# Another order in the first DMA queues and on TensorE, and 8 picked rows in place of 14 for the second tile

## The chip, the cores and the metric

The kernel runs on one core of one Trainium2 chip. A core has TensorE (PE in the profile, its weight loads PEld), VectorE (DVE), ScalarE (ACT), GpSimd (POOL) and SyncE (SP), and 16 DMA engines. SP and ACT issue plain DMAs (SPq and ACTq in the rows), POOL issues the gathers. The metric is the device time of one launch in microseconds; smaller is better.

## The reference

A recommendation model for a batch of 1024. For each sample, 32 embedding rows of 16 floats are looked up in 32 tables, then three interaction layers follow, and a small tower on the sums:

```
e = stack([tbl_m[ids[:, m]] for m in range(32)], axis=1)            # (1024, 32, 16)
x0 = xk = e
for W in (W0, W1, W2):                                              # (32, 32 or 64, 64)
    xk = relu(einsum('bmd,bhd,mhk->bkd', x0, xk, W))
    outs.append(sum(xk, axis=2))
h = concatenate([concatenate(outs, 1), dense_ctx], 1)               # 3 * 64 + 16 = 208 wide
y = relu(relu(h @ W_top1 + b_top1) @ W_top2 + b_top2) @ W_top3
```

The tables have 1000, 1250, 12500 or 125000 rows. Everything is float32.

## The kernel before

**Tiles and phases.** The batch is cut into 8 tiles of 128 samples, each tile into two sides A and Bs of 64 samples. A phase is one layer of one side of one tile; `PHASES` lists all 48 in the order in which every engine goes through them. It begins (0, layer 0, A), (0, layer 1, A), (0, layer 0, Bs), (0, layer 2, A), (0, layer 1, Bs); the text calls these phases 0 to 4. A phase of layer 1 or 2 has 16 steps, a phase of layer 0 has 4.

**A step.** VectorE (L1110) multiplies a 128x1024 block of the current layer (`xk`, in PSUM) with a block of the replicated first layer (`x0rep`, in SBUF) into `z`, and TensorE (L753) contracts `z` with a block of the weights into `acc`. Some steps have their product made by GpSimd (L554, `z_pool`). `z` is a ring of 6 buffers, so VectorE can be 6 products ahead of TensorE. After a phase ScalarE takes `acc` through the relu into `xk_copy` (L861) and fills the two halves ("turns") of `xk` for a later phase: `fill_first` (L823) and `fill_second` (L842, L847). Phase 1 alone takes its first turn straight from `acc` (L831 on ScalarE, L1094 on VectorE).

**Where the embeddings come from.** GpSimd gathers rows with indirect DMAs (L504), one per table and tile, 32 per tile. At the start that would take long, so for tables of 1000 or 1250 rows the first two tiles are partly *picked*: SP and ACT load the whole table as 125 lines of 8 or 10 rows (L385, into the part of `x0rep` that is still free), and for each group of three or four tables TensorE spreads the line numbers over the partitions (`spread_lines`, L648), VectorE turns them into ones and zeros (`find_lines`, L1004), TensorE selects the lines by a product (`pick`, L662), and VectorE masks the other rows away and adds up (`find_rows` L1019, `clear_others` L1031, `take_rows` L1044). `PICKS` lists the groups: 6 for tile 0 (20 tables), then 4 for tile 1 (14 tables). The last three picks stand on VectorE between the four products of phase 0 (`between`).

**Saving and replicating.** The rows of a tile go from `emb` to DRAM (`x0_rows`; L457 for tile 0, L405 later) and are read back replicated as `x0rep` (L428, eight "slots" of 512 KB a side), as `lay` (L414) and as `squares` (L420). Tile 0 is saved in two parts: the even tables by `save_first(0)`, which waits for 3 pick groups, and the odd ones by `save_first(1)`, which waits for all 6. The even slots are loaded after the first part, the odd slots, on which the third product of phase 0 waits, after the second.

**Weights.** `w0` is symmetrised on VectorE (L1064), written to DRAM twice (L400, `w0_twice`) and read back rotated by 16 small loads (L379; `W0_LOADS` of them on ACT's queue, the rest on SP's). `w1` and `w2` are brought in by 8 direct loads (`STRAIGHT`) and 4 loads (`WRAPPED`) from a scratch copy in DRAM that two DMAs make first (`make_wrap`, L765); all of that is issued by ACT, the part for `w2` between two of its phases (L931 to L937). TensorE starts phase 1 only with all 12 loads of `w1` in, and phase 3 only with all of `w2`.

**What sets the order.** Each engine runs its own program in the order in which it is written, with semaphores between them. A DMA issued by SP or ACT stands in that engine's program like any other instruction: what is behind it waits until it is issued.

## Time and profile before

| | |
|---|---|
| median of 3 runs | 629.13 us (628.42 to 631.07) |
| profiled execution, its own time | 629.63 us |
| its span | 627.7 us |
| VectorE busy | 577.4 us, 92% |
| TensorE busy | 585.6 us, 93% |
| GpSimd busy | 497.3 us, 79% |
| ScalarE busy | 349.6 us, 56% |

The difference between the execution's own time and its span, 1.9 us, lies around the span. Busy time of TensorE is modelled. Read the table with the timeline beside it: an engine that is 92% busy over the whole span can still be mostly idle in its first tenth.

### The profile page before, as it was taken

The page shows a single profiled execution, that of the slowest core. Times are in us where ns is not written, and L with a number is a line of the kernel's source. Part 1 is how long each engine was busy: PE and PEld are TensorE (multiplying, and loading weights), DVE is VectorE, ACT ScalarE, POOL GpSimd, SP SyncE. Part 2 cuts the span into 40 slices and gives each one's busy share as a digit, 9 for nine tenths or more (in the row PEclk, how much of TensorE's full clock was granted, in tenths as well). Part 3 has the DMA queues.
Part 4 walks back from the last instruction along what each step waited for, and adds up shares of the span by engine and source line. Part 5 has one row for each costly group of instructions (what it writes and reads, how often), then busy time and mean ns, then how long its engine had stood idle before and what let it go on. Part 6 is the DMA issues. An engine that isn't in the chain of part 4 may idle for free. (4 is left out here: it accounts for less than half of the span.)

```text
span 627.7 us, 8728 instructions
## 1 busy us (share of the span) xinstructions
PE 585.6 (93%) x3126; PEld 214.1 (34%) x3126; DVE 577.4 (92%) x582; ACT 349.6 (56%) x535; POOL 497.3 (79%) x349
## 2 busy tenths in 40 slices
PE   3485689999999899999999999999999999999998
PEld 3361223222442224322342224322442234333444
DVE  5567599899999999999999999999999999999993
ACT  0105174745755667635755666635755666756741
POOL 6753579799888988899888988898888896668770
PEclk9879979999999999999999999999999999999999
DMA  4689979940499928993599727980699728990000
GB/s 110 129 165 236 251 119 272 294 118 4 77 237 224 191 19 185 231 240 58 81 243 247 159 28 198 296 210 3 114 236 242 138 28 202 237 247 3 1 2 1
DMA packets 89326, 95.36 MB, mean 152 GB/s; under 512 B 59597, under 2 KB 68338, under 8 KB 89282
## 3 DMA queue, kind: packets, MB, share of 16 engines
q1 hardware_dynamic: 78590, 90.55, 62.8%
q0 software_dynamic: 7104, 1.83, 3.9%
q10 hardware_dynamic: 3588, 2.41, 1.5%
q8 instruction: 25, 0.41, 0.3%
q14 instruction: 19, 0.16, 0.1%
HBM read 91.35 MB, written 3.94 MB: 152 GB/s over the span
## 5 line engine op out<-in xcount | busy, mean ns | idle before, releaser
L1110 DVE TENSOR_TENSOR z<-xk,x0rep 128x1024 f32<-128x1024 f32 x457 | 522.9, 1223 | 19.8 <-issue 9.6
L753 PE MATMUL acc<-z,w_sb 128*64 128x512 f32 x1828 | 433.6, 599 | 20.4 <-DVE z L1110 17.3
L554 POOL TENSOR_TENSOR z_pool<-x0rep,xk_copy 128x1024 f32<-128x1024 f32 x119 | 283.3, 2381 | 55.7 <-PE acc L753 27.9
L504 POOL DMA_INDIRECT emb<-tbl,idx x222 | 213.0, 959 | 58.4 <-issue 48.3
L753 PEld LDWEIGHTS acc<-z,w_sb 128*64 128x64 f32 x1828 | 123.7, 137 | 294.9 <-issue 161.2
L847 ACT ACTIVATE xk<-xk_copy 32x1024 f32<-32x1024 f32 x128 | 130.5, 1019 | 94.3 <-DVE z L1110 93.1
L753 PE MATMUL acc<-z_pool,w_sb 128*64 128x512 f32 x476 | 122.5, 593 | 0.0
L861 ACT ACTIVATE xk_copy<-acc 64x512 f32<-64x512 f32 x128 | 75.2, 588 | 3.7 <-PE acc L753 2.2
L842 ACT ACTIVATE xk<-lay 128x1024 f32<-128x1024 f32 x15 | 15.4, 1027 | 75.7 <-DVE z L1110 75.7
L753 PEld LDWEIGHTS acc<-z_pool,w_sb 128*64 128x64 f32 x476 | 33.7, 137 | 65.1 <-issue 62.8
L823 ACT ACTIVATE xk<-xk_copy 128x1024 f32<-128x1024 f32 x31 | 31.9, 1028 | 14.2 <-DVE z L1110 13.9
L1083 DVE TENSOR_REDUCE row_sums<-layer_out 128x32 f32<-128x512 f32 x47 | 32.2, 684 | 0.0
L805 ACT ACTIVATE squares<-squares 32x1024 f32<-32x1024 f32 x16 | 16.8, 1050 | 23.4 <-issue 14.5
L867 ACT ACTIVATE layer_out<-acc 128x512 f32<-128x512 f32 x47 | 27.8, 591 | 2.1 <-PE acc L753 1.4
L879 ACT ACTIVATE in<-row_sums 64x32 f32<-64x32 f32 x94 | 21.3, 227 | 4.7 <-DVE row_sums L1083 3.6
L1031 DVE TENSOR_TENSOR x0rep<-acc,mask 128x480 f32<-128x480 f32 (+1 forms) x10 | 6.7, 666 | 14.2 <-PE acc L662 14.2
L662 PE MATMUL acc<-x0rep 125*128 125x160 f32 (+1 forms) x68 | 14.8, 377 | 4.9 <-DMA x0rep<-tbl 4.9
L749 PE MATMUL acc<-squares,w0d_sb 128*64 128x512 f32 x64 | 16.9, 606 | 0.4
L823 ACT ACTIVATE xk<-lay 128x1024 f32<-128x1024 f32 x15 | 15.4, 1028 | 2.8 <-DMA lay<-x_rows 2.4
L784 ACT ACT_TABLE_LOAD x1 | 1.3, 1283 | 27.5 <-issue 27.5
L662 PEld LDWEIGHTS acc<-x0rep 125*128 125x128 f32 x68 | 12.6, 259 | 7.9 <-DMA x0rep<-tbl 5.3
L590 PEld LDWEIGHTS top<-h,wt_sb 128*64 128x64 f32 x224 | 12.7, 137 | 4.0 <-issue 4.0
(67 smaller groups left out, 140.6 us busy)
## 6 DMA issues: line engine op xcount, KB each, us to landing
x0rep<-x_rows SPq DMA_DIRECT2D x128, 512.0 KB, 20.7
lay<-x_rows SPq DMA_DIRECT2D x30, 512.0 KB, 6.9
emb<-tbl,idx POOLq DMA_INDIRECT x222, 3.5
squares<-x_rows SPq DMA_DIRECT2D x16, 128.0 KB, 8.6
x_rows<-emb SPq DMA_DIRECT2D x7, 256.0 KB, 4.6
x_rows<-emb SPq DMA_DIRECT2D x9, 128.0 KB, 5.9
w_wrap<-w ACTq DMA_DIRECT2D x4, 128.0 KB, 9.7
w_sb<-w ACTq DMA_DIRECT2D x8, 64.0 KB
```

What stands on the lines that cost most here:

```text
L504: pool.indirect_dma_start(out=emb[:, i % 2, m, :], out_offset=None, in_=tables[m], in_offset=bass.IndirectOffsetOnAxis(ap=idx[:, i, m:m + ...
L554: pool.tensor_mul(z_pool[:, (count - 1) % POOL_RING, :], x0rep[:, g % X0_GROUPS, slot, :], xk_copy[:, side, :]).then_inc(z_pool_ready, 1)
L662: op = pe.matmul(acc[:, ACC_AT[q], t * n * D:(t + 1) * n * D], hots[:, q % HOTS, t * P:(t + 1) * P], lines[:, ALL_PICKED.index(m), 0:n * D ...
L749: pe.matmul(bank[c * H:(c + 1) * H, :], w0d_sb[:], squares[:, side, c * COLS:(c + 1) * COLS], start=False, stop=False)
L753: mm = pe.matmul(bank[c * H:(c + 1) * H, :], w[:, tile, :], src[:, c * COLS:(c + 1) * COLS], start=(k == 0), stop=last)
L823: act.activation(xk[:, 0, :], src, ACT.Copy).then_inc(xk_ready[0], 1)
L847: op = act.activation(xk[q * Q:(q + 1) * Q, 1, :], xk_copy[other * Q:(other + 1) * Q, side, :], ACT.Copy)
L861: op = act.activation(xk_copy[half * H:(half + 1) * H, side, c * COLS:(c + 1) * COLS], bank[c * H:(c + 1) * H, :], ACT.Relu)
L867: act.activation(layer_out[:, n % OUTS, :], bank, ACT.Relu).then_inc(acc_taken, 1)
L879: op = act.activation(dst[:, at:at + ROWS], row_sums[c * H:(c + 1) * H, i % 2, row, :], ACT.Copy)
L1083: dve.tensor_reduce(row_sums[:, i % 2, SUM_ROWS.index((layer, side)), :], layer_out[:, n % OUTS, :].rearrange("p (b d) -> p b d", d=D), AX ...
L1110: dve.tensor_mul(z[:, (count - 1) % RING, :], xk[:, bank, :], src).then_inc(z_ready, 1)
```

## The change

It touches only what is issued in about the first 80 us of the program.

- *SP's queue*: the lines of pick groups 0 and 1 stand ahead of where they stood, and `w0_twice` ahead of the lines of groups 2 to 5. The indices of tile 1 come by a load of their own (`idx_second_in`), those of tiles 2 to 7 at the end of the first block. The two copies for `w1_wrap` come from ACT's queue to the end of that block, the two for `w2_wrap` from ACT's queue to the place ahead of the loads of side Bs. Two of the rotated `w0` loads move in between the first save and its wait, two more go to ACT (`W0_LOADS` 12).
- *ACT's queue*: of the eight direct `w1` loads four stand behind the second `copy_rows`, and the four wrapped ones behind the first `square`. The copies are gone from it.
- *TensorE*: `pick(3)`, `pick(4)` and `pick(5)` stand ahead of where they stood.
- *VectorE*: the ids of tile 1 are split after three picks instead of before the first.
- *Tile 1*: 8 tables picked (two groups) and 24 gathered, in place of 14 and 18.

```diff
-PICKS = [(0, g) for g in range(6)] + [(1, g) for g in range(4)]
+PICKS = [(0, g) for g in range(6)] + [(1, g) for g in range(2)]
...
-W0_LOADS = 10
+W0_LOADS = 12
...
             sp.dma_start(idx[:, 0, :], ids[0:P, :]).then_inc(idx_first_in, 16)
+            load_lines(sp, False, 0)
             for dst, src in ((w0a_sb, w0a), (w0b_sb, w0b)):
                 sp.dma_start(dst, src).then_inc(w0ab_in, 16)
-            load_lines(sp, False, 0)
-            sp.dma_start(idx[:, 1:NT, :], ids[P:B, :].rearrange("(t p) m -> p t m", p=P)).then_inc(idx_in, 16)
-            for g in range(1, len(PICKED)):
-                load_lines(sp, False, g)
+            sp.dma_start(idx[:, 1, :], ids[P:2 * P, :]).then_inc(idx_second_in, 16)
+            load_lines(sp, False, 1)
             sp.wait_ge(w0_summed, 2)
             for n in range(2):
                 sp.dma_start(w0_twice[:, n, :].rearrange("q (r t k) -> q r t k", r=M, t=TILES0), w0a_sb).then_inc(w0_twice_in, 16)
+            for g in range(2, len(PICKED)):
+                load_lines(sp, False, g)
+            make_wrap(sp, w1_wrap, w1, w1_wrap_in)
+            sp.dma_start(idx[:, 2:NT, :], ids[2 * P:B, :].rearrange("(t p) m -> p t m", p=P)).then_inc(idx_in, 16)
...
-                sp.wait_ge(saved_first, 32 * (odd + 1))
             save_first(0)
+            sp.wait_ge(w0_twice_in, 32)
+            load_w0(sp, W0_LOADS, W0_LOADS + 2)
+            sp.wait_ge(saved_first, 32)
             for slot in range(0, SLOTS, 2):
                 load_x0(0, A, slot)
-            load_w0(sp, W0_LOADS, TILES0 * P // M)
+            load_w0(sp, W0_LOADS + 2, TILES0 * P // M)
             save_first(1)
+            sp.wait_ge(saved_first, 64)
...
+            make_wrap(sp, w2_wrap, w2, w2_wrap_in)
             load_side(0, Bs)
...
@@ scalar
-            load_w0(act, 0, W0_LOADS - 2)
+            load_w0(act, 0, 8)
             copy_rows(0)
-            load_w0(act, W0_LOADS - 2, W0_LOADS)
-            make_wrap(w1_wrap, w1, w1_wrap_in)
-            load_w(w1_sb, w1.tensor, TILES, w1_in, STRAIGHT)
+            load_w0(act, 8, W0_LOADS)
+            load_w(w1_sb, w1.tensor, TILES, w1_in, STRAIGHT[:2])
             copy_rows(1)
-            act.wait_ge(w1_wrap_in, 32)
-            load_w(w1_sb, w1_wrap, WRAP, w1_in, WRAPPED)
+            load_w(w1_sb, w1.tensor, TILES, w1_in, STRAIGHT[2:])
...
             square(0, A)
+            act.wait_ge(w1_wrap_in, 32)
+            load_w(w1_sb, w1_wrap, WRAP, w1_in, WRAPPED)
...
                 if n == 1:
-                    make_wrap(w2_wrap, w2, w2_wrap_in)
@@ vector
-            dve.wait_ge(idx_in, 16)
-            split_ids(1)
             for q in range(7):
+                if q == 3:
+                    dve.wait_ge(idx_second_in, 16)
+                    split_ids(1)
                 pick_rows(q)
...
-            between = {1: 7, 2: 8, 4: 9}
+            between = {1: 7}
```

SP's queue from the first index load to the second save, before (`z<-w0a` is the load of `w0`, `w_twice` the doubled `w0`, `x0rep<-tbl` the lines of the picked tables, `x_rows<-emb` the two saves):

```order
L391 DMA idx<-ids 128x32
L393 DMA z<-w0a 128x256
L393 DMA z<-w0b 128x256
L385 DMA x0rep<-tbl 125x128 x2
L395 DMA idx<-ids 128x7x32
L385 DMA x0rep<-tbl 125x128 x2
L385 DMA x0rep<-tbl 125x160 x6
L400 DMA w_twice<-z 4x32x256 [waits w0_summed]
L400 DMA w_twice<-z 4x32x256
L457 DMA x_rows<-emb 128x16x16 [waits picked_out,gathered_first0]
L457 DMA x_rows<-emb 128x8x16
L428 DMA x0rep<-x_rows 128x1x1024 [waits saved_first]
```

The same stretch of SP's queue now:

```order
L398 DMA idx<-ids 128x32
L392 DMA x0rep<-tbl 125x128 x2
L401 DMA z<-w0a 128x256
L401 DMA z<-w0b 128x256
L402 DMA idx<-ids 128x32
L392 DMA x0rep<-tbl 125x128 x2
L406 DMA w_twice<-z 4x32x256 [waits w0_summed]
L406 DMA w_twice<-z 4x32x256
L392 DMA x0rep<-tbl 125x160 x6
L385 DMA w_wrap<-w 128x256 x2
L410 DMA idx<-ids 128x6x32
L467 DMA x_rows<-emb 128x16x16 [waits picked_out,gathered_first0]
```

The two scratch copies of `w1` and the indices of tiles 2 to 7 now stand directly ahead of the first save; the large index load no longer stands ahead of the lines of group 1.

ScalarE from the first `copy_rows` to the take-over of phase 0, before:

```order
L784 ACTIVATE lay<-xk 16x1024 [waits rows_turned]
L379 DMA w_sb<-w_twice 16x2x64 x2
L765 DMA w_wrap<-w 128x256 x2
L776 DMA w_sb<-w 64x1x256 x2
L776 DMA w_sb<-w 32x1x256 x4
L776 DMA w_sb<-w 64x1x256 x2
L784 ACTIVATE lay<-xk 16x1024 [waits rows_turned]
L776 DMA w_sb<-w_wrap 32x1x256 [waits w1_wrap_in]
L776 DMA w_sb<-w_wrap 32x1x256 x3
L805 ACTIVATE squares<-squares 32x1024 [waits rows_in0]
L831 ACTIVATE xk<-acc 64x512 [waits step_done]
```

And now:

```order
L789 ACTIVATE lay<-xk 16x1024 [waits rows_turned]
L380 DMA w_sb<-w_twice 16x2x64 x4
L781 DMA w_sb<-w 64x1x256 x2
L781 DMA w_sb<-w 32x1x256 x2
L789 ACTIVATE lay<-xk 16x1024 [waits rows_turned]
L781 DMA w_sb<-w 32x1x256 x2
L781 DMA w_sb<-w 64x1x256 x2
L808 ACTIVATE squares<-squares 32x1024 [waits rows_in0]
L781 DMA w_sb<-w_wrap 32x1x256 [waits w1_wrap_in]
L781 DMA w_sb<-w_wrap 32x1x256 x3
L836 ACTIVATE xk<-acc 64x512 [waits step_done]
```

The four wrapped `w1` loads have moved behind an ACTIVATE that waits for the squares of the second save.

ScalarE between the second turn of phase 1 (the `xk<-xk_copy` rows) and phase 2 (the `squares` and `lay` rows), before:

```order
L847 ACTIVATE xk<-xk_copy 32x1024 x3
L765 DMA w_wrap<-w 128x256 x2
L776 DMA w_sb<-w 64x1x256 [waits x0_in0_7]
L776 DMA w_sb<-w 64x1x256
L776 DMA w_sb<-w 32x1x256 x4
L776 DMA w_sb<-w 64x1x256 x2
L776 DMA w_sb<-w_wrap 32x1x256 [waits w2_wrap_in]
L776 DMA w_sb<-w_wrap 32x1x256 x3
L937 DMA in<-ctx_t 16x128
```

And now:

```order
L852 ACTIVATE xk<-xk_copy 32x1024 x3
L781 DMA w_sb<-w 64x1x256 [waits x0_in0_7]
L781 DMA w_sb<-w 64x1x256
L781 DMA w_sb<-w 32x1x256 x4
L781 DMA w_sb<-w 64x1x256 x2
L781 DMA w_sb<-w_wrap 32x1x256 [waits w2_wrap_in]
L781 DMA w_sb<-w_wrap 32x1x256 x3
L941 DMA in<-ctx_t 16x128
L808 ACTIVATE squares<-squares 32x1024 [waits rows_in1]
```

The two copies are gone from here, and the semaphore `w2_wrap_in` on which the wrapped loads wait is now raised by copies that SP issued earlier.

## Rows read from the trace of the kernel before

**Rows 1.** The page: busy time of each engine, its share and instructions.

```profile
PE 585.6 (93%) x3126; PEld 214.1 (34%) x3126; DVE 577.4 (92%) x582; ACT 349.6 (56%) x535; POOL 497.3 (79%) x349
```

**Rows 2.** Timeline, VectorE, 35 to 120: start, duration, operation, idle before.

```profile
35.42 0.66 DVE L1031 TENSOR_TENSOR x0rep<-acc,mask 128x480 f32<-128x480 f32 x1 [9.87 <-PE acc L662]
...
48.37 2.36 DVE L1110 TENSOR_TENSOR z<-xk,x0rep 128x1024 f32<-128x1024 f32 x2 [0.36 <-DMA x0rep<-x_rows]
...
54.22 4.62 DVE L1110 TENSOR_TENSOR z<-xk,x0rep 128x1024 f32<-128x1024 f32 x4
61.53 5.75 DVE L1110 TENSOR_TENSOR z<-xk,x0rep 128x1024 f32<-128x1024 f32 x5 [2.69 <-issue]
...
67.79 3.48 DVE L1110 TENSOR_TENSOR z<-xk,x0rep 128x1024 f32<-128x1024 f32 x3
78.15 4.62 DVE L1110 TENSOR_TENSOR z<-xk,x0rep 128x1024 f32<-128x1024 f32 x4 [6.88 <-issue]
82.97 9.14 DVE L1110 TENSOR_TENSOR z<-xk,x0rep 128x1024 f32<-128x1024 f32 x8 [0.20 <-ACT xk L823]
```

**Rows 3.** Timeline, ScalarE and its DMA issues (ACTq), 20 to 100.

```profile
41.88 2.60 ACTq L776 DMA_DIRECT2D w_sb<-w_wrap  x4
49.55 1.05 ACT L805 ACTIVATE squares<-squares 32x1024 f32<-32x1024 f32 x1 [6.66 <-DMA squares<-x_rows]
...
56.88 0.56 ACTq L765 DMA_DIRECT2D w_wrap<-w  x1
...
60.96 3.11 ACTq L776 DMA_DIRECT2D w_sb<-w  x4
68.05 2.60 ACTq L776 DMA_DIRECT2D w_sb<-w_wrap  x4
70.68 5.23 ACTq L937 DMA_DIRECT2D in<-ctx_t  x1
...
78.94 2.38 ACT L861 ACTIVATE xk_copy<-acc 64x512 f32<-64x512 f32 x4
```

**Rows 4.** Timeline, DMA issues of SP, 0 to 60.

```profile
20.20 1.39 SPq L457 DMA_DIRECT2D x_rows<-emb  x2
24.42 3.66 SPq L428 DMA_DIRECT2D x0rep<-x_rows  x4
...
37.91 2.63 SPq L457 DMA_DIRECT2D x_rows<-emb  x2
42.94 0.55 SPq L428 DMA_DIRECT2D x0rep<-x_rows  x1
43.52 0.67 SPq L420 DMA_DIRECT2D squares<-x_rows  x1
```

**Rows 5.** Windows: stretch, busy times, TensorE clock, DMA share, GB/s.

```profile
18.00:20.00 2.00, 0.29 (x3) 0.05 (x1) 2.00 (x5) 0.00 (x0) 1.39 (x2) 1.00 0.31 100
26.00:38.00 12.00, 6.51 (x20) 3.29 (x21) 2.41 (x6) 2.29 (x2) 9.02 (x10) 0.53 1.00 222
...
42.00:44.00 2.00, 2.00 (x17) 1.35 (x18) 1.93 (x5) 0.88 (x1) 0.82 (x1) 1.00 0.06 18
46.00:77.00 31.00, 20.46 (x90) 5.88 (x88) 21.65 (x24) 10.28 (x13) 14.36 (x9) 1.00 1.05 245
```

**Rows 6.** The page, DMA issues: count, size, median us to landing.

```profile
x0rep<-x_rows SPq DMA_DIRECT2D x128, 512.0 KB, 20.7
```

**Rows 7.** Timeline, TensorE, 72 to 90.

```profile
72.30 1.03 PE L753 MATMUL acc<-z,w_sb 128*64 128x512 f32 x4
79.52 5.39 PE L753 MATMUL acc<-z,w_sb 128*64 128x512 f32 x12 [6.19 <-DVE z L1110]
...
87.36 2.79 PE L753 MATMUL acc<-z,w_sb 128*64 128x512 f32 x12 [0.70 <-DMA w_sb<-w_wrap]
```

**Rows 8.** Timeline, GpSimd, 40 to 160.

```profile
39.97 0.94 POOL L504 DMA_INDIRECT emb<-tbl,idx  x1 [0.30 <-issue]
...
56.84 2.37 POOL L554 TENSOR_TENSOR z_pool<-x0rep,xk_copy 128x1024 f32<-128x1024 f32 x1 [12.71 <-ACT xk_copy L861]
```

23 lines of the change are left out of this document (10 added, 13 removed).

## The prediction

> **What bounds the kernel now.** I read the page first. VectorE is 92% and TensorE 93% busy [rows 1], so over the whole span the two products per step leave no room, and the change removes none of them. What can move is idle time near the start. The second view is VectorE's timeline up to 120 us: it shows where the most loaded engine still waits [rows 2]. Three waits matter. At 35.42 it has been idle 9.87 us for the last pick of tile 0. At 61.53 it waits 2.69 us for ScalarE to fill the second turn of phase 1; nothing in the change touches that. At 78.15 it starts phase 2 after 6.88 us of idle. From 82.97, where phase 3 starts, it hardly stops. So the result is read from two marks: S, the start of phase 1 (54.22), and T, the start of phase 3 (82.97). What T moves by, the end moves by, since everything behind it is released by the same engines in the same order.
>
> The third view, ScalarE's timeline, explains 78.15 [rows 3]: from 56.88 ScalarE issues w2's two copies, then eight loads until 64.07 (60.96 + 3.11), then waits until 68.05 for the copies to land, then issues four more and the context load until 75.91 (70.68 + 5.23). Only then come the squares and the fill of phase 2. The fourth, SP's issues, gives the chain before S [rows 4]: second save issued at 37.91, landed at 42.94, slot 1 issued there, third product at 48.37 after a wait of 0.36 us for that slot [rows 2]; then two products, the last step of phase 0 on TensorE, the turn-over, and S. From slot 1's issue to S it is 54.22 - 42.94 = 11.3 us. The fifth view, the windows, tells that DMA is full from 26 to 38 (share 1.00, 222 GB/s), nearly empty from 42 to 44 (0.06), and full again from 46 to 77 (1.05) [rows 5].
>
> **The change, part by part.** My working starts from the profiled execution, 629.63 us (span 627.7 and 1.9 around it), 0.5 above the median of 629.13.
>
> *Picks.* Two groups fewer, and the last pick of tile 0 is not behind `select_rows(0)` any more. That takes the 9.87 us wait away: following VectorE, with the durations that the operations have now, the sixth group would be done at about 26 us instead of 37.84. This is no gain by itself, because the save it releases stands in SP's queue behind other transfers. The two picks dropped (8 and 9) lie between products of phase 0 that wait for slot 1 anyway. I cost all of this at 0; with the DMA cover gone it is the first rival.
>
> *Six more gathers.* One takes 0.94 and a gap of 0.30 [rows 8], so 6 x 1.25 = 7.5 us of GpSimd, against the 12.71 us that it now stands idle before its first product. Cost 0; the cover left is 5 us.
>
> *First save.* SP can issue it somewhat earlier than now (20.20), but the rings are still busy then: from 18 to 20 table lines are still being moved at 100 GB/s [rows 5], and their amount is unchanged. The copies of w1, 2 x 128 KB, now stand ahead of the save: 0.26 MB at 222 GB/s are 1.2 us. So the even slots start at 24.42 + 1.2 = 25.6. Bounds: if the save did not queue at all it would land 4.2 us (24.42 - 20.20) after an issue at about 18, that is at 22, 2.4 us sooner than now; at the other end two copies at 100 GB/s cost 2.6 us. I take +1.2, since a transfer issued into a busy queue lands late here (median 20.7 us for a slot [rows 6]).
>
> From 18 to 20 the DMA share is 0.31 at a time when almost only table lines are moving [rows 5]. The Trainium skill ("DMA: Bandwidth & Descriptors", section on why a DMA increments its semaphore by 16 and not by 1) says that a transfer is spread over the largest number of engines up to 16 that divides both outer dimensions; a table of 125 lines gets 5, and 5 of 16 is 0.31, so the trace agrees. By that rule the save queues on those five engines only; by an even spread the queue would be empty and the first term would be the 22 us bound, 3.6 us better than what I take.
>
> *Second save.* SP issues it at about 30.5 now (25.6, four slots in 3.66 [rows 4], two small loads), far ahead of 37.91. But the even slots are ahead of it in the same queue. From 26 to 38 DMA moved 12 us x 222 GB/s = 2.7 MB: four even slots (2.1), two copies (0.26), eight w1 loads (0.38). Now the copies are gone and four of the w1 loads (0.19) are issued later: 0.45 MB less, 2.0 us. Drained at 38 + 1.2 - 2.0 = 37.2, the save landed 4.2 us later (as the first did), at 41.4: 1.5 us sooner than 42.94. Slot 1 then has no wrapped w1 loads beside it (41.88 now [rows 3]), 128 KB or 0.5 us. Sum for S: -2.0, S = 52.2. Bounds: -7 (the first rival) and +1.4 (2.6 for the copies, none of the 2.0 given back, minus the 1.2 counted, is 42.94 + 1.4).
>
> *Wrapped w1 loads.* They were issued at 41.88 into an empty stretch. Now they follow the squares of tile 0, which were taken up at 49.55, 6.0 us after their issue at 43.52; with slot 1 at 41.4 they are issued from 48.0, into the full stretch. TensorE wants them at S + 1.3 = 53.5. How long they take there no row tells directly. Nearest above: w2's wrapped loads, issued at 68.05, released TensorE at 87.36, 19.3 us later, but with eight loads still ahead of them. Nearest below: 6.0 us for the squares. I take 8, nearer to the lower end, because the queue ahead is short: TensorE starts phase 1 at 56.0, after some 5 us of idle. After such an idle it runs at half clock: three steps (12 records) took 5.39 us from 79.52 after 6.19 us of waiting, against 2.79 us for three from 87.36 [rows 7]. So 5.4 + 13 x 0.93 = 17.5 us, and phase 1 ends on TensorE at 73.5. VectorE is not held up, it can be 6 products ahead.
>
> *w2 off ScalarE's path.* Two issues (1.2 us) and the wait for the copies (64.07 to 68.05, 4.0) go. ScalarE has the rest issued at 75.91 - 5.2 - 2.0 = 68.7 or sooner, and VectorE ends phase 1 at S + 17.05 = 69.3 (71.27 now [rows 2]). So phase 2 follows at once, or within 1.5 us, and the 6.88 us wait goes almost whole. What is late next is the take-over of phase 1 for phase 3: now L861 starts at 78.94 and VectorE's phase 3 4.0 us later, at 82.97. It now has to wait for TensorE's end of phase 1 (73.33 in the old trace, no bound there [rows 7]). T = 73.5 + 4.0 = 77.5, that is -5.5. Bounds of T - S, 28.75 now: 23.1 with w1 in time (19.1 + 4.0), 28.75 with nothing won.
>
> *w2's landing.* TensorE starts phase 3 now at 87.36, after waiting for the last of w2 [rows 7], 30.5 us after 56.88, with 768 KB on ACT's queue. Now 512 KB from about 55: by bytes 20.3 us, 75 to 76; by transfers, 12 of 14, 26.1 us, 81. It is wanted at T + 1.2 = 78.7. I take 0.5 us of loss out of a range of 0 to 2.3.
>
> Sum: -5.5 + 0.5 = -5.0; 629.63 - 5.0 = 624.6 for the profiled execution, 624.1 against the median.
>
> **The rivals.**
>
> *First: the start is won whole.* If the second save overtakes the even slots in the queue, it lands about 5.5 us after 30.5, slot 1 is issued at 36 instead of 42.94 and S moves by -6.9 to 47.3. The wrapped w1 loads then come early too, T - S is 23.1, T = 70.4 (-12.6); w2, wanted at 72 and there at about 74, takes 2 back: -10.6, 618.5. GpSimd allows it: 24 gathers of 1.25 us after the first twelve end near 49, its first product is wanted at S + 2.6 = 49.9. For it speaks that the picks really are done at 26; against it the 20.7 us of [rows 6]. The Trainium skill (same page, "Queues, rings and completion order") has descriptors of one queue consumed in order on each engine, and the semaphore raised only after every earlier write of that engine: by that this rival falls, and no row here shows two transfers overtaking.
>
> *Second: the start gains nothing and w2 becomes the wait.* The copies of w1 cost 2.6 us, S stays at 54.2, and phase 3 on TensorE starts at 84.9 instead of 87.36 because the wrapped loads of w1 are ahead of w2 in ACT's queue. Result -2.5, 626.6: no change that can be told. For it: the full DMA stretch from 46 on, in which the same bytes have to move in any order.
>
> *Third, the slower side: the wrapped w1 loads are as late as w2's.* With 19.3 us instead of 8 they release TensorE at 67.3; phase 1 ends at 84.8, T = 88.8, +5.9, 635.0. The place is TensorE's first product of phase 1; it decides from a landing 13.4 us after issue (release at 61.4, phase 1's end at 78.9, T at 82.97 as now). Against it: in their place there is little ahead on ACT's queue. For it: SP's queue is as full as it was then. By the Trainium skill's rule on the number of engines, cited above, such a load with an outer dimension of 4 runs on 4 of the 16 engines, which makes long landings likelier; no row here shows single engines.
>
> **How the numbers follow.** Forecast (S -2, T -5 to -6): 0.52, own range 620.5 to 627. First rival 0.13. Second 0.24. Third, with milder forms of it, 0.11. Predicted 624.1. The range, 617.5 to 630, holds the first two rivals and leaves most of the third out. 0.5% is 3.1 us, about what a measurement of this kernel can tell from no change: faster means below 626.0. Of the forecast 0.45 lies there, all of the first rival, 0.04 of the second: 0.62. Slower (above 632.3) is most of the third: 0.09. The rest, 0.29, is the same.
>
> **What would show it.** Second save: SP's first odd slot at 41.4 (rival one: 36; rival two: 43 or later). S at 52.2. VectorE's wait before phase 2 under 2 us. TensorE's first product of phase 1 released by the w1 loads, not by VectorE, at about 56, and at half clock; rival three has it at 67. T at 77.5, TensorE's phase 3 at 79 to 81. GpSimd idle before its first product some 5 us. From phase 3 on the trace should be the old one, shifted. The forecast is wrong if S moves by more than 5 us, if VectorE still waits over 4 us before phase 2, or if a new wait for x0rep or for gathered rows appears in phases 3 to 8.

## The result, and the profile after

After 633.53 us (median of 7 runs, 632.22 to 634.11), before on the same chip 630.17 us (median of 7, 628.42 to 632.04): ratio 1.0047, 95% interval 1.003 to 1.0064. That is 0.5% slower, small but clear of the noise. The forecast was 624.1 us, five below the kernel before, with a range of 617.5 to 630; it came out three above the kernel before. The execution whose profile follows took 634.11 us, span 632.3.

VectorE's timeline after, in the columns of [rows 2]:

```profile
48.06 2.36 DVE L1114 TENSOR_TENSOR z<-xk,x0rep 128x1024 f32<-128x1024 f32 x2 [11.39 <-DMA x0rep<-x_rows]
54.77 1.42 DVE L1098 TENSOR_SCALAR xk<-acc 64x512 f32<-64x512 f32 x2 [4.36 <-PE acc L764]
56.23 4.62 DVE L1114 TENSOR_TENSOR z<-xk,x0rep 128x1024 f32<-128x1024 f32 x4
63.54 2.36 DVE L1114 TENSOR_TENSOR z<-xk,x0rep 128x1024 f32<-128x1024 f32 x2 [2.69 <-issue]
69.01 1.23 DVE L1114 TENSOR_TENSOR z<-xk,x0rep 128x1024 f32<-128x1024 f32 x1 [3.11 <-PE acc L764]
...
74.00 8.07 DVE L1114 TENSOR_TENSOR z<-xk,x0rep 128x1024 f32<-128x1024 f32 x7
87.47 9.14 DVE L1114 TENSOR_TENSOR z<-xk,x0rep 128x1024 f32<-128x1024 f32 x8 [5.40 <-ACT xk L828]
```

S, the start of phase 1, is 56.23 (54.22 before), T, the start of phase 3, 87.47 (82.97). The wait of 6.88 us before phase 2 is gone: the seven products from 74.00 run without a gap from the end of phase 1 through phase 2. But 3.11 us appear inside phase 1 and 5.40 before phase 3, both for TensorE in the end. Its own timeline, with [rows 7] to compare:

```profile
39.76 3.68 PE L764 MATMUL acc<-z,w_sb 128*64 128x512 f32 x8 [4.36 <-DMA w_sb<-w_twice]
49.34 1.98 PE L764 MATMUL acc<-z,w_sb 128*64 128x512 f32 x4 [5.90 <-DVE z L1114]
...
67.00 6.95 PE L764 MATMUL acc<-z,w_sb 128*64 128x512 f32 x20 [12.27 <-DMA w_sb<-w_wrap]
...
89.37 2.79 PE L764 MATMUL acc<-z,w_sb 128*64 128x512 f32 x12 [1.69 <-DMA w_sb<-w_wrap]
```

TensorE stood idle 12.27 us for a wrapped load of w1 and began phase 1 at 67.00. ScalarE and its queue (against [rows 3]) tell when that load was issued:

```profile
49.31 1.06 ACT L808 ACTIVATE squares<-squares 32x1024 f32<-32x1024 f32 x1 [15.90 <-DMA squares<-x_rows]
49.32 2.60 ACTq L781 DMA_DIRECT2D w_sb<-w_wrap  x4
...
64.39 7.08 ACTq L781 DMA_DIRECT2D w_sb<-w_wrap  x4
71.51 2.56 ACTq L941 DMA_DIRECT2D in<-ctx_t  x1
...
83.43 2.40 ACT L866 ACTIVATE xk_copy<-acc 64x512 f32<-64x512 f32 x4 [4.88 <-PE acc L764]
```

Issue at 49.32, release 17.7 us later; the take-over of phase 1 starts at 83.43 as soon as TensorE is through, and phase 3 follows 4.04 us behind. SP's issues (against [rows 4]) and the windows (against [rows 5]: stretch, busy times, TensorE's granted clock, DMA share, GB/s):

```profile
21.08 1.39 SPq L467 DMA_DIRECT2D x_rows<-emb  x2
...
25.33 3.54 SPq L438 DMA_DIRECT2D x0rep<-x_rows  x4
...
30.40 8.60 SPq L467 DMA_DIRECT2D x_rows<-emb  x2
42.57 0.55 SPq L438 DMA_DIRECT2D x0rep<-x_rows  x1
```

```profile
18.00:20.00 2.00, 2.00 (x9) 1.92 (x8) 1.22 (x4) 0.00 (x0) 1.39 (x3) 1.00 0.86 225
26.00:38.00 12.00, 9.38 (x64) 5.88 (x64) 8.44 (x15) 1.01 (x1) 9.00 (x10) 0.85 1.01 205
42.00:44.00 2.00, 1.44 (x4) 0.00 (x0) 0.00 (x0) 0.00 (x0) 1.39 (x3) 0.50 0.19 21
46.00:77.00 31.00, 15.39 (x48) 4.71 (x50) 17.92 (x17) 11.32 (x14) 17.12 (x12) 0.64 1.05 230
```

The second save is issued 7.5 us earlier than before and lands 0.4 us earlier. DMA is as full from 46 to 77 as before (1.05), and TensorE's mean clock in that stretch is 0.64 where it was 1.00. GpSimd, against [rows 8]:

```profile
48.73 0.94 POOL L518 DMA_INDIRECT emb<-tbl,idx  x1 [0.30 <-issue]
58.85 2.35 POOL L569 TENSOR_TENSOR z_pool<-x0rep,xk_copy 128x1024 f32<-128x1024 f32 x1 [9.18 <-ACT xk_copy L866]
```

From T to the end of the span it is 544.8 us, before 544.7. The two agree so closely partly by chance. The shift against before is 4.5 us at T, but ScalarE's take-overs show 3.8 at 195.61 (before: 191.84), 2.4 at 217.16 (214.74) and 4.5 again at 289.66 (285.15). In between each kernel waits for a landing of `x0rep` that the other does not wait for, first before, then after:

```profile
207.82 11.41 DVE L1110 TENSOR_TENSOR z<-xk,x0rep 128x1024 f32<-128x1024 f32 x10 [1.11 <-DMA x0rep<-x_rows]
```

```profile
280.50 1.23 DVE L1114 TENSOR_TENSOR z<-xk,x0rep 128x1024 f32<-128x1024 f32 x1 [1.01 <-DMA x0rep<-x_rows]
282.74 11.41 DVE L1114 TENSOR_TENSOR z<-xk,x0rep 128x1024 f32<-128x1024 f32 x10 [1.01 <-DMA x0rep<-x_rows]
```

Fourteen of the twenty profiles of this document have such waits behind 150 us, of 0.2 to 1.1 us each and at changing places. So a mark near the start tells the end of a single profile to 1 or 2 us, not better.

### The profile page after: what moved, and what is told of

Same layout as the page of the kernel before. It is cut to its first block and busy times, and to the rows that moved or that the text cites. A ratio compares the mean times of both kernels' runs of the same rounds, so it can differ in the third digit from the quotient of the medians.

```text
span 632.3 us, 8682 instructions
## 1 busy us (share of the span) xinstructions
PE 586.2 (93%) x3108; PEld 213.3 (34%) x3108; DVE 573.3 (91%) x572; ACT 349.9 (55%) x535; POOL 502.9 (80%) x355
## 5 line engine op out<-in xcount | busy, mean ns | idle before, releaser
L1114 DVE TENSOR_TENSOR z<-xk,x0rep 128x1024 f32<-128x1024 f32 x457 | 523.3, 1226 | 33.2 <-DMA x0rep<-x_rows 13.7
L518 POOL DMA_INDIRECT emb<-tbl,idx x228 | 218.7, 959 | 58.2 <-issue 50.9
L808 ACT ACTIVATE squares<-squares 32x1024 f32<-32x1024 f32 x16 | 16.8, 1051 | 29.3 <-DMA squares<-x_rows 18.4
L677 PE MATMUL acc<-x0rep 125*128 125x128 f32 (+1 forms) x56 | 13.2, 408 | 5.8 <-DMA x0rep<-tbl 5.8
L760 PE MATMUL acc<-squares,w0d_sb 128*64 128x512 f32 x64 | 17.7, 631 | 0.3
L605 PE MATMUL top<-h,wt_sb 128*64 128x128 f32 x224 | 13.4, 273 | 0.0
## 6 DMA issues: line engine op xcount, KB each, us to landing
squares<-x_rows SPq DMA_DIRECT2D x16, 128.0 KB, 19.3
```

Source lines behind the costliest of these rows:

```text
L518: pool.indirect_dma_start(out=emb[:, i % 2, m, :], out_offset=None, in_=tables[m], in_offset=bass.IndirectOffsetOnAxis(ap=idx[:, i, m:m + ...
L605: last = pe.matmul(top[halves[half], m * P:(m + 1) * P], wt2_sb[:, k, columns_of(m, half)], h1[:, k, :], start=(k == 0), stop=(k == F1 // ...
L677: op = pe.matmul(acc[:, ACC_AT[q], t * n * D:(t + 1) * n * D], hots[:, q % HOTS, t * P:(t + 1) * P], lines[:, ALL_PICKED.index(m), 0:n * D ...
L1114: dve.tensor_mul(z[:, (count - 1) % RING, :], xk[:, bank, :], src).then_inc(z_ready, 1)
```

## The experiments

Eighteen more runs followed in five groups; the kernels of a group share one chip and its runs of the kernel before. The chips were of two kinds. On the chips of two groups the kernel before takes 630 us, as on the first one; on three it takes 654 to 656, and there TensorE is held up some 20 us in the picks (last section). I call them the 630 and the 654 chips; ratios are each against before on the same chip. The marks of all profiles, to which the paragraphs below refer (us from the span's start; "w1" is the issue of its first wrapped load and TensorE's first product of phase 1, V where VectorE released it; "PE 3" TensorE's first product of phase 3, "~" where it is read inside a merged row):

```
                       slot 1    S      w1 issue, first product     T      PE 3    span    ratio
630 chips
before                 42.94   54.22   41.88   55.59  V           82.97   87.36   627.7
after                  42.57   56.23   49.32   67.00  17.7        87.47   89.37   632.3   1.0047
eight_picked_alone     43.47   57.48   40.88   58.84  V           86.01  ~88.8    629.9   1.0022
top_later_alone        43.38   54.69   42.15   56.06  V           81.16  ~84.6    625.4   0.9989
skewed_top_later       42.28   55.53   48.90   58.94  10.0        79.19   84.12   624.6   0.998
both_and_top_later     42.79   54.29   41.32   55.66  V           79.18   81.89   622.1   0.9972
after_ten_picks_2      43.76   56.81   49.85   66.32  16.5        87.01   89.80   630.5   1.0045
all_mended_2           41.76   54.61   47.77   56.83   9.1        77.82   82.93   623.9   0.997
654 chips
before_marks           67.10   79.92   64.26   81.30  V          107.89 ~110.6    653.6
after_marks            67.18   78.51   73.42   90.19  16.8       110.30  115.74   661.2   1.0064
w1_before_square       66.28   78.17   70.88   91.82  20.9       112.57  113.94   658.1   1.0062
w1_before_square_2     64.97   77.52   70.23   92.16  21.9       111.62  113.00   657.7   1.0085
w1_behind_square       68.73   81.22   74.98   94.27  19.3       114.59  115.96   661.0   1.006
w1_loads_plain_rows    65.51   78.24   71.70   85.03  13.3       104.44  112.62   659.7   1.0019
w2_copies_by_sp        68.99   82.47   65.00   83.84  V          105.67  114.55   657.9   1.0034
after_skewed           67.17   78.47   73.28   83.00   9.7       103.37  110.63   655.3   1.002
w2_by_sp_skewed        64.70   75.93   63.50   77.30  V           99.14  108.43   653.8   1.0004
after_filled           66.06   90.31   72.24   94.01  21.8       114.31  115.69   660.4   1.0087
after_ten_picks        58.36   71.36   64.67   80.63  16.0       101.17  105.08   648.8   0.9959
all_mended             57.45   70.23   63.47   73.28   9.8        93.43   98.55   641.9   0.9844
```

My theory for the first four runs below: the late wrapped loads of w1 end phase 1 (rival three), and the rest of the change gains what it should. Its rival: w2, or the DMA volume, binds anyway. Each profile is one execution, and slot 1 moves by over 4 us between profiles of kernels with the same first queues on the 654 chips, so single marks are read against the nearest row and the ratios against their intervals.

**w1_behind_square.** The kernel before with w1's wrapped loads alone moved, as the change has them:

```diff
             copy_rows(1)
-            act.wait_ge(w1_wrap_in, 32)
-            load_w(w1_sb, w1_wrap, WRAP, w1_in, WRAPPED)
...
             square(0, A)
+            act.wait_ge(w1_wrap_in, 32)
+            load_w(w1_sb, w1_wrap, WRAP, w1_in, WRAPPED)
```

> The kernel before with the other part alone: its four wrapped w1 loads stand behind the square of tile 0 (issue near 49.6 instead of 41.9). Theory: they release TensorE 15 to 19 us after issue, near 66 instead of 55.6, at half clock, phase 1 ends on TensorE near 83, T near 87, so 4 us slower than before, 634. Rival (in the changed kernel the loads were late because of the copies of w2 and w1 on SP's queue): release near 58, T as before, no change in time.

659.95 us, ratio 1.006 (1.0029 to 1.0091). This one edit is slower by about as much as the whole change (3.9 us in the medians, 3.4 and 4.3 for the whole). TensorE's release, 19.3 us after the issue:

```profile
94.27 6.79 PE L753 MATMUL acc<-z,w_sb 128*64 128x512 f32 x20 [14.56 <-DMA w_sb<-w_wrap]
```

**w1_before_square** and, on another chip, **w1_before_square_2**: the kernel after with the same two lines moved back ahead of `square(0, A)`.

> The changed kernel with one thing put back: the four wrapped w1 loads are issued ahead of the square of tile 0 (right behind the other four direct ones, near 35 us) instead of behind it (49.32). Theory (the loads, issued 14 us later into full DMA queues, cost the time): TensorE's first product of phase 1 waits for VectorE and not for w1, at S + 1.3; phase 1 ends on TensorE near S + 19, T = S + 23 to 24, that is 79 to 80 in place of 87.5, and the whole is about 7 us faster than the changed kernel, 626 to 627, and 0.4 to 0.7% faster than before. Rival (the loss is in the start itself: cold TensorE, late slot 1, and the w1 loads only take the blame): T stays over 84 and the time within 2 us of the changed kernel's 633.5.

> The kernel w1_before_square again, for a chip on which the second layout is ready before slot 1 is issued: there the four wrapped loads of w1 are issued at about 35 in place of 49, ahead of the odd x0 slots. Theory (the loads are late since they stand behind the odd slots and side B): they are down before phase 0 ends, TensorE starts phase 1 with VectorE's first product at about 57, T at about S + 25, and what is left is w2's hold before phase 3: ratio 0.998 to 1.003 against after's 1.005. Rival (these loads are late wherever they stand): release over 15 us after issue or TensorE's first product of phase 1 after 60, ratio 1.004 to 1.007.

659.92 us, 1.0062 (1.0036 to 1.0089), and 659.24 us, 1.0085 (1.0052 to 1.0118). Both fell on 654 chips, where the second layout is late, so that the loads came out only some 5 us behind slot 1's issue, and not 14 us earlier as meant. There they took 20.9 and 21.9 us and released TensorE no sooner than in after_marks (91.82 and 92.16 against 90.19, on three chips). A place 1 to 1.6 us nearer to the issue of slot 1, but still behind it, gains nothing; what an issue well ahead of the slots would do in the new order stays untested. In the old order the loads are issued 1.1 to 4.0 us ahead of slot 1 (all rows with V), and in all of them VectorE released TensorE, 14 to 19 us after the issue; when the loads had landed these rows do not show.

**w1_loads_plain_rows.** The kernel after, w1's wrapped loads reading 32 plain rows instead of 4 groups of 8. The rows then come from other tiles of the scratch copy, so this kernel leaves out part of `w1`; it serves for the time alone.

```diff
                         rows = bass.AP(src, ((odd * H + h) * tiles + t) * H,
+                                       [[tiles * H, (hi - lo) * PER_GROUP], [1, half * H]] if plain else
                                        [[(PER_GROUP * tiles + 1) * H, hi - lo], [tiles * H, PER_GROUP], [1, half * H]])
...
-            load_w(w1_sb, w1_wrap, WRAP, w1_in, WRAPPED)
+            load_w(w1_sb, w1_wrap, WRAP, w1_in, WRAPPED, plain=True)
```

> The changed kernel with the wrapped w1 loads reading the same number of bytes as plain rows (32 rows of 1 KB, one outer dimension of 32 on both sides, in place of 4 groups of 8 rows); they read other tiles of the scratch, so part of w1 is not what the reference has. Everything else is the same. Theory (a load with an outer dimension of 4 uses 4 engines, 8 rows after one another on each, and each row waits its turn beside SP's rows): the four loads are spread over all engines and land some 4 to 6 us after issue, TensorE starts phase 1 near 56 instead of 67, T near 80, time near 627. Rival (they are late because the queues as a whole are full, whatever the engines): release stays at 15 us or more after issue and the time at 633.

657.82 us, 1.0019 (0.9986 to 1.0051). Release 13.3 us after issue, between the theory's 4 to 6 and the rival's 15; T 104.44. But the end gained less than T: TensorE was held before phase 3 by w2 (the "hold" in what follows).

```profile
112.62 5.39 PE L764 MATMUL acc<-z,w_sb 128*64 128x512 f32 x12 [7.97 <-DMA w_sb<-w_wrap]
```

**w2_copies_by_sp.** The kernel before with w2's two DRAM copies on SP's queue, behind the odd slots, instead of ScalarE's:

```diff
+            for at, t in ((0, TILES - WRAP // 2), (WRAP // 2, 0)):
+                sp.dma_start(bass.AP(w2_wrap, ...), w2[:, t:t + WRAP // 2, :]...)   # ahead of load_side(0, Bs)
...
                 if n == 1:
-                    make_wrap(w2_wrap, w2, w2_wrap_in)
```

> The kernel before with one part of the change alone: the two copies into the scratch of w2 are issued by SP ahead of the loads of side Bs, not by ScalarE. Theory of the prediction: ScalarE loses two issues and its wait of 4 us, VectorE's wait of 6.9 us before phase 2 shrinks to under 2, T goes from 83 to about 78, the time falls by about 5 us to 625. Rival (the issues of ScalarE are held back by its full queue whatever their number): the context load is still issued until near 75, T stays within 1.5 us and so does the time.

659.16 us, 1.0034 (1.0003 to 1.0066): slower, if barely clear of the noise, though the part did what it was priced for. VectorE's wait before phase 2 is 1.09 us and T - S 23.2 us, close to the 23.1 of the prediction's bound. The gain is given back at phase 3:

```profile
100.60 4.62 DVE L1111 TENSOR_TENSOR z<-xk,x0rep 128x1024 f32<-128x1024 f32 x4 [1.09 <-PE acc L756]
105.67 6.88 DVE L1111 TENSOR_TENSOR z<-xk,x0rep 128x1024 f32<-128x1024 f32 x6 [0.45 <-ACT xk L826]
116.57 1.22 DVE L1111 TENSOR_TENSOR z<-xk,x0rep 128x1024 f32<-128x1024 f32 x1 [4.02 <-PE acc L756]
```

```profile
114.55 4.58 PE L756 MATMUL acc<-z,w_sb 128*64 128x512 f32 x12 [7.34 <-DMA w_sb<-w_wrap]
```

So T is the wrong mark where TensorE is held for long. VectorE may run 6 products into phase 3 (the x6) while TensorE waits for w2. The end goes more closely with TensorE's first product of phase 3: from it to the end of the span it is 543.0 to 547.1 in the twelve profiles of 654 chips, while from T it is up to 10 us more in one 654 profile than in another (545.5 in w1_before_square, 555.3 in w1_loads_plain_rows). On the 630 chips, where the holds are shorter, the two marks do about equally well: 540.2 to 542.9 from TensorE's product and 542.9 to 546.1 from T. The kernel after itself is the profile that TensorE's mark fits worst: its phase 3 on TensorE starts 2.0 us later than before's and its span is 4.6 longer, of which some 2 us are the late waits for `x0rep` shown above.

**before_marks, after_marks.** The two kernels unchanged, for their marks on a 654 chip.

> The kernel before, as it is, for its marks on this chip beside the others: its VectorE should start phase 1 and phase 3 about 28.8 us apart and wait some 7 us before phase 2; its TensorE should not wait for a load of w2 by over 1 us before phase 3. All theories say so.

> The kernel after, as it is, on this chip. Theory (the wrapped loads of w1 are late and end phase 1): ratio 1.003 to 1.007, TensorE's first product of phase 1 released by a wrapped load of w1 some 15 to 20 us after its issue. Rival (the loss comes from a cold TensorE in phase 0 alone): the same ratio, but the load is down before phase 0 is left. Rival (chance of the one chip): ratio 1.000.

655.43 us in one run, with the marks 28.0 us apart and 6.10 us of wait before phase 2, as expected; and 659.2 us, 1.0064 (1.0036 to 1.0091). After is slower by the same share here, with the same wait of TensorE for w1 (13.19 us), though here S came 1.4 us earlier than in before_marks. The later S of the first chip is thus no condition for the loss.

**after_skewed, w2_by_sp_skewed.** To have plain rows and the right numbers, the DRAM copies were written with each group of 8 rows one tile lower, in after and in w2_copies_by_sp:

```diff
-                queue.dma_start(bass.AP(wrap, at * H, [[WRAP * H, P], [1, WRAP // 2 * H]]),
-                                src[:, t:t + WRAP // 2, :].rearrange("p t k -> p (t k)")).then_inc(done, 16)
+                queue.dma_start(bass.AP(wrap, at * H, [[(PER_GROUP * (WRAP + 1) - 1) * H, GROUPS], [(WRAP + 1) * H, PER_GROUP], [1, WRAP // 2 * H]]),
+                                src[:, t:t + WRAP // 2, :].rearrange("(g e) t k -> g e (t k)", e=PER_GROUP)).then_inc(done, 16)
...
+                        if tiles == WRAP:
+                            rows = bass.AP(src, ((odd * H + h) * (WRAP + 1) + t - (odd * H + h) // PER_GROUP) * H,
+                                           [[(WRAP + 1) * H, (hi - lo) * PER_GROUP], [1, half * H]])
```

> The kernel after, with the two DRAM copies of w1 and of w2 written with each group of 8 rows one tile lower, so that the eight wrapped loads (4 groups x 8 rows before) read 32 plain rows; the result is the same. Theory (a load whose slowest dimension is 4 goes through few DMA engines and is late in a full stretch): TensorE is released into phase 1 about 13 us after the issue in place of 17 to 21, w2's wait before phase 3 (2 to 8 us) goes too, and the time is 4 to 8 us under the kernel after's, so at or below the time before: ratio 0.993 to 0.999. Rival (the bytes ahead in the queues decide, not the form): release still 17 to 21 us after issue, ratio as after's, 1.003 to 1.007.

> The kernel before with w2's DRAM copies issued by SyncE behind the odd x0 slots in place of ScalarE, and both DRAM copies skewed as in after_skewed. The copies by SyncE alone gave 1.0034, with VectorE's wait before phase 2 gone and TensorE held 7.3 us by a wrapped load of w2. Theory: with loads of plain rows that hold shrinks to under 2 us and the 5 us of the closed wait reach the end: ratio 0.991 to 0.996. Rival (the DMA engines are full from phase 0 to phase 3, and what lands earlier only pushes something else): ratio 1.000 to 1.004 with the hold at another transfer.

656.26 us, 1.002 (0.9993 to 1.0047), and 656.09 us, 1.0004 (0.9973 to 1.0035). For w1 the theory held, with a smaller delay than its 13 us: 9.7 us from issue to release against 16.8 in after_marks on the same chip, with the same amount of data, slot 1 issued at the same time (67.17 and 67.18) and the loads too (73.28 and 73.42). The whole, with w2's loads changed too, is 2.9 us shorter than after_marks, but its ratio stays above the 0.993 to 0.999 expected.

```profile
73.28 1.97 ACTq L784 DMA_DIRECT2D w_sb<-w_wrap  x4
```

```profile
83.00 6.84 PE L764 MATMUL acc<-z,w_sb 128*64 128x512 f32 x20 [6.04 <-DMA w_sb<-w_wrap]
...
110.63 4.97 PE L764 MATMUL acc<-z,w_sb 128*64 128x512 f32 x12 [7.05 <-DMA w_sb<-w_wrap]
```

For w2 it fell: TensorE still waited 7.05 us, and 8.93 in w2_by_sp_skewed, over 20 us after the wrapped loads were issued (86.93 and 84.11). The T of w2_by_sp_skewed is 8.8 us ahead of before_marks, its phase 3 on TensorE some 2 us (4.0 us of the 8.8 it had at S already). What stands before w2 there is volume: DMA shares of 1.03 to 1.31 in every window of 4 us from 68 to 108, and 57 GB/s from 108 to 112. The next three runs tested that.

**both_and_top_later, top_later_alone, skewed_top_later.** The six loads of the top layers' weights (928 KB, first used in tile 1) moved from behind side Bs to behind the save of tile 1's rows, in w2_by_sp_skewed, in before and in after_skewed:

```diff
             load_side(0, Bs)
-            sp.dma_start(wt1_sb[:, 0, :], wt1[0:P, :]).then_inc(top_in, 16)      # and five more
...
                 save_x0(i, 0, X_ROWS - M, M, x0_saved[i % 2])
+                if i == 1:
+                    sp.dma_start(wt1_sb[:, 0, :], wt1[0:P, :]).then_inc(top_in, 16)      # and five more
```

> w2_by_sp_skewed, and the six loads of the top layers' weights (928 KB, not used before tile 1) issued behind the save of tile 1's rows in place of behind the loads of side B. Theory (the DMA engines are full from the odd x0 slots to the landing of w2, at some 240 GB/s, so w2 lands when the bytes ahead of it are through): 3.9 us fewer bytes ahead, TensorE's phase 3 starts some 4 us earlier than in w2_by_sp_skewed, ratio 0.993 to 0.997. Rival (w2's wrapped loads are late for a reason of their own, their queue's order or form): phase 3 starts as there, ratio 0.999 to 1.004.

> The kernel before, with only the six top-layer loads moved as in both_and_top_later. Theory: w2's copies and loads still come behind ScalarE's fills, VectorE still waits some 6 us before phase 2 because ScalarE is busy issuing; fewer bytes ahead shorten the issue of ScalarE's stalled DMAs a little (up to 3 us): ratio 0.995 to 1.001. Rival (the bytes are the only bound, also of the kernel before): ratio 0.993 to 0.995, as much as with both.

> after_skewed with the six top-layer loads moved as in both_and_top_later. Theory: w1's release a little earlier than 13 us after issue or the same, w2's hold before phase 3 (7 us there) shrinks by some 4 us: ratio 0.995 to 0.999, 3 to 4 us under after_skewed's 1.002. Rival (queue order): 1.001 to 1.004.

627.86 us, 0.9972 (0.9951 to 0.9993); 629.63 us, 0.9989 (0.9967 to 1.001); 628.81 us, 0.998 (0.9959 to 1.0002), all on one 630 chip. The rows go the way of the volume theory: from slot 1's issue to TensorE's phase 3 it is 39.1 us in both_and_top_later and 41.8 in skewed_top_later, against 43.7 and 43.5 with the loads in their old place. These pairs come from different kinds of chip, so the 4.6 and 1.6 us are a direction more than a size, and the two ratios (0.9972 where 0.993 to 0.997 was expected, and 0.998) have no run beside them on the same chip with the loads in their old place. The one comparison on one chip, top_later_alone against before, cannot be told from no change; there ScalarE's issues still hold VectorE for 4.61 us. The first of the three is a version that beats the kernel before by a small margin:

```profile
79.18 9.14 DVE L1114 TENSOR_TENSOR z<-xk,x0rep 128x1024 f32<-128x1024 f32 x8 [3.33 <-ACT xk L829]
```

```profile
81.89 2.80 PE L756 MATMUL acc<-z,w_sb 128*64 128x512 f32 x12 [2.51 <-DMA w_sb<-w_wrap]
```

**eight_picked_alone.** The kernel before with the split alone: `PICKS` with two groups for tile 1, `between = {1: 7}`, the picks 8 and 9 and their spreads gone.

> The kernel before with only the split of the second tile changed: 8 rows picked and 24 gathered in place of 14 and 18; all queues and orders as before. The prediction's terms for this part (picks 0, gathers 0): ratio 0.998 to 1.002. Rival (the picks filled waits of TensorE, which now falls to the lower clock in phase 0): S 1 to 3 us later, ratio 1.002 to 1.005. Rival (more gathers delay GpSimd's first product or tile 1): GpSimd's first product later than ScalarE's copy allows, ratio above 1.002.

630.97 us, 1.0022 (0.9997 to 1.0047): not told from no change, but S is 57.48, 3.3 us later than before's, and the rows say why:

```profile
50.73 1.98 PE L749 MATMUL acc<-z,w_sb 128*64 128x512 f32 x4 [3.95 <-DVE z L1105]
...
54.20 1.76 PE L749 MATMUL acc<-z,w_sb 128*64 128x512 f32 x4
```

```profile
48.00:54.00 6.00, 3.27 (x8) 0.96 (x10) 2.35 (x2) 1.06 (x1) 1.11 (x2) 0.57 1.03 211
```

The same window of both_and_top_later, on the same chip and with ten pick groups:

```profile
48.00:54.00 6.00, 3.11 (x14) 0.68 (x12) 5.04 (x6) 2.19 (x3) 0.00 (x0) 1.00 1.02 252
```

The granted clock is 0.57 against 1.00. Without the two picks TensorE stands idle 3.95 us for slot 1, is granted the 1.2 GHz level for most of the window, and its third step takes 1.98 us for four matmuls, which take 1.08 in before. From VectorE's third product to S it is 8.0 us here, 5.9 in both_and_top_later and in before, 8.2 in after. The remaining 1.1 us is the third product itself (49.45 for 48.37), which waited for slot 1.

Three parts of the change, each alone on the kernel before, gave 1.006, 1.0034 and 1.0022; the whole is 1.0047 to 1.0064. They don't add up, and the last of them has 1 in its interval. A likely reason, not tested, is that all three push against the same landings before phase 3.

**after_filled.** The kernel after with work for TensorE in that wait:

```diff
                 for k, (who, tile, _, _) in enumerate(STEPS[n]):
+                    if (n, k) == (0, 2):
+                        for _ in range(28):
+                            pe.matmul(top[:, 0:TILES0 * H], ident_f[:], w0_sb[:].rearrange("p t k -> p (t k)"), start=True, stop=True)
```

> The kernel after, with 28 matmuls on TensorE (its own weights times the identity, into a bank that nobody reads again) in its wait between the second and the third product of phase 0. Theory of the cold clock: the third product and the squares run at 1.1 us in place of 1.9, VectorE's wait for the end of phase 0 is 0.5 to 2 us in place of 4.4, so S some 2 to 3 us earlier than the kernel after's (56.2 where slot 1 is issued at 42.6); T and the end gain nothing, since the late loads of w1 end phase 1: ratio as after's, 1.003 to 1.007. Rival (S's delay reaches the end): ratio 1.000 to 1.002. Rival (not the clock but the length of the work): S as after's or later.

659.48 us, 1.0087 (1.0058 to 1.0117). It did not test the clock: it ran on a 654 chip, where slot 1 is waited for less than 1 us, so the filling was pure delay, and its 28 matmuls were longer than I had worked out. It did show something else. VectorE waited 13.93 us for the end of phase 0 (2.04 in after_marks) and S was 90.31, 11.8 us later than in after_marks, on another chip; T was 4.0 later, TensorE's phase 3 at 115.69 against 115.74, the span 0.8 shorter. A start that is 12 us late vanishes before phase 3: in after_marks the landings of w1 and w2 set that mark, not S. Whether filling the wait would keep the clock up and bring S forward stays untested.

**after_ten_picks**, on a 654 chip, and **after_ten_picks_2**, on a 630 chip. The kernel after with four groups for tile 1 again (`range(4)`, `between = {1: 7, 2: 8, 4: 9}`, the picks 8 and 9 behind `select_rows(1)`).

> The kernel after with before's split of the second tile: 14 rows picked and 18 gathered, the two last pick groups where they stood. Theory (the two groups kept TensorE from its lower clock while it waited for slot 1): S 2 to 3.5 us earlier than after's 56.2, at about 53 to 54; w1's loads still end phase 1, so T 85 to 87.5 and ratio 1.001 to 1.006. Rival (the picks cost VectorE its own time in phase 0): S no earlier than after's.

> after_ten_picks again, for a chip without the stall of some 20 us in TensorE's picks. There (theory of the cold clock): from VectorE's third product to S 5.9 us in place of after's 8.2, S 53.5 to 54.5; w1's wrapped loads still released at about 66, so T 85 to 87 and ratio 1.001 to 1.005. On a chip with the stall: the gathers end 7.5 us earlier with six fewer of them, slot 1 is issued at about 58 in place of 66, ratio 0.993 to 0.999 as in the first run.

650.4 us, 0.9959 (0.9931 to 0.9987), and 632.4 us, 1.0045 (1.0026 to 1.0064): faster than before on the one kind of chip, slower on the other. On the 630 chip my expectation of S fell: 56.81, not 53.5 to 54.5, and 7.7 us from the third product to S, not 5.9. The new order has all of TensorE's picks done by 38, the two restored ones too, and nothing is left for the wait:

```profile
50.43 1.97 PE L768 MATMUL acc<-z,w_sb 128*64 128x512 f32 x4 [6.19 <-DVE z L1119]
```

From 48 to 54 the granted clock is 0.50. So the lower clock in phase 0 appears with either part alone, the split or the earlier order; before's late picks were TensorE's cover. The ratio is that of the kernel after: on a 630 chip this part does not carry the loss.

**all_mended**, on a 654 chip, and **all_mended_2**, on a 630 chip. after_ten_picks with the skewed copies and the top loads later.

> The kernel after with all that the runs point to: ten pick groups as before, skewed DRAM copies of w1 and w2, the top layers' weights behind the save of tile 1. It differs from both_and_top_later (0.9972) in the first DMA queues and in w1's place alone. Theory (the first queues gain nothing once slot 1 is issued at the same time, and w1 behind the square costs nothing once its loads are plain): ratio 0.995 to 0.999. Rival (the queues' order costs by itself): 1.000 to 1.003. Rival (it gains): below 0.995.

> all_mended again. On a chip without the stall: S about 54, T about 78 to 79.5, w2's hold before phase 3 some 3 us, ratio 0.994 to 0.998, as both_and_top_later (0.9972). On a chip with the stall: 0.981 to 0.988, as in the first run.

643.31 us, 0.9844 (0.9814 to 0.9875), and 627.63 us, 0.997 (0.9945 to 0.9995). This version beats both kernels on both kinds of chip. Against after_ten_picks on the same chips it is 7.1 and 4.8 us shorter: that is what plain rows and 928 KB later are worth together. On the 630 kind it is level with both_and_top_later (0.9972), which has before's first queues: there the new first queues and the later place of w1's loads together are worth nothing, neither way.

## Why the prediction was wrong

It failed at one large term, the time that w1's wrapped loads take to land. It had w2's landing and its mark wrong as well, and what happened was the third rival, nearly to its numbers.

*Wrapped w1 loads: the step that failed.* "I take 8, nearer to the lower end, because the queue ahead is short." It was 17.7 us; in eight profiles with these loads behind slot 1 in their old form it was 16.0 to 21.9. The sum for T was 48.0 + 8 + 17.5 + 4.0 = 77.5; it became 49.3 + 17.7 + 16.4 + 4.0 = 87.4 (read: 87.47). The other three terms were right to 1.3 us. The row of w2, 19.3 us, was the near one, and I had set it aside because of eight loads ahead of it on ACT's queue. Those were not what made it long: here none stood ahead. Rival three's release was 67.3, measured 67.00; its T was 88.8, its time 635.0 against 633.53. I had given it 0.11. What had spoken against it was the queue of the issuing engine. What the runs show to count is the form of the load (16.8 us against 9.7 with plain rows); that the rest comes from the full DMA engines, which the row 46 to 77 had shown, fits all rows but was not tested by itself for w1. By the rule of the Trainium skill cited in the prediction ("DMA: Bandwidth & Descriptors", section on why a DMA increments its semaphore by 16 and not by 1), 4 groups of 8 rows go over 4 engines and 32 rows over 16; the measured 16.8 against 9.7 us on one chip goes the way of the rule, though no row here shows single engines. By the rule 128 KB at 245 GB/s take 2.1 us over 4 of 16 engines and 0.5 over all, an estimate that is short of the 7 us measured; where the rest comes from is open, and so is why plain rows took 13.3 us in w1_loads_plain_rows and 9.1 to 10.0 in the four with skewed copies.

*Second save.* Right in the issue (30.40 for 30.5) and in the queue that kept it back (first rival out: slot 1 at 42.57, not 36). Slot 1 was to be issued 1.5 us earlier than before and came 0.4 earlier. From 26 to 38 DMA moved 205 GB/s where it had moved 222, so 0.45 MB fewer were not 2.0 us less.

*S.* "From slot 1's issue to S it is 11.3 us" was taken over unchanged and became 13.7. From the third product to S the granted clock was 0.58 where before had 1.00, and that stretch took 8.2 us for 5.9. The prediction counted picks as 0 because they lie in waits. They did, and that was their worth. S came 2.0 late in place of 2.0 early. By the trace of this chip that cost nothing in the end, since TensorE's phase 1 hung on w1 whose issue does not wait for S.

*w2 off ScalarE's path.* Right by the experiments: T - S is 23.2 in w2_copies_by_sp and in both profiles of all_mended, with w1 in time or nearly so, for a bound of 23.1. In the kernel after itself the wait before phase 2 went partly by luck. ScalarE was through with its issues at 74.07, 17.8 us behind S where 16.5 was forecast, because the four wrapped loads took 7.08 us to issue in place of 2.60; VectorE, held in phase 1, came later still. With VectorE at the forecast's S + 17.05 some 3 us of wait would have been left, an estimate from these rows and the 2.2 us that before takes from ScalarE's square to phase 2.

*w2's landing, and "what T moves by, the end moves by".* This is the second error, hidden in the kernel after by the first. I had w2 down at 75 to 81 and took 0.5 us of loss out of 0 to 2.3. It released TensorE at 89.37. The forecast had scaled before's 30.5 us, from ScalarE's first issue for w2 to the release, with what was left on ScalarE's queue, by bytes to 20.3 or by transfers to 26.1. But it stayed 30.5 (58.90 to 89.37): taking the two copies off that queue did not shorten it. So even with w1 in time TensorE could not have started phase 3 of this kernel before 89.37, 2.0 us later than before, unless w2 had landed sooner as well. On the 654 chips the hold before phase 3 was 7 to 9 us in the four profiles that had T early and the top weights in their old place, and w2_copies_by_sp, the very part from which 5.5 us were to come, was slower than before. Had the 8 us been right, the result would likely have been near the second rival's, not the forecast's: on the 654 chip after_skewed has T 4.5 us earlier than before_marks, and 1.002.

*First save, gathers, GpSimd.* Even slots at 25.33 (forecast 25.6); GpSimd idle 9.18 us (5), since its product waits for a later S; the gathers cost nothing here. *Half clock* at the start of phase 1: as forecast, a granted clock of 0.59 from 67 to 73. "VectorE is not held up" was wrong with the later release: 3.11 us at 69.01. *The rest of the trace* was the old one, shifted by 2.4 to 4.6, with the waits for `x0rep` at other places.

*The range.* Its upper end, 630, left out a mechanism that I had priced with its own rows. Between two rows for the same kind of load, 6.0 and 19.3 us, the case for the long one (same form, same full engines) was better than 0.11.

## What to carry to other kernels

When DMA is full through a stretch, ask of each transfer in it how much is ahead of it on the engines, not on its own queue, and put first what is needed first: here moving 928 KB that nobody needed yet, together with reading plain rows, gained 5 to 7 us. Where one engine can run ahead of another, read the start of a phase on both: the one that can run ahead says little while the other is held for data. And before work is taken out of a wait because it "costs nothing there", look whether it keeps TensorE's clock up.
